# A graph-attention and expert kernel: a small GpSimd fill is put behind every row gather, in a chain

## What is computed

```python
ft = (layernorm(x) @ W).reshape(n, 4, 64)
e = leaky_relu(e_src[src] + e_dst[dst], 0.2)       # a score for each edge and head
a = softmax of e over the edges of one dst, * dist
x = x + segment_sum(ft[src] * a, dst)
x = x + top-2 of 6 experts(layernorm(x))           # three 256x256 layers in each expert
```

## Time and profile before

| what | value |
|---|---|
| median of 3 runs | 4007.06 us (4005.75 to 4013.24) |
| the profiled execution: its own time | 4011.02 us |
| its span, first to last instruction | 4009.3 us |
| mean granted TensorE clock | 0.77 of full speed |
| the gathers of `main_stage` | 1,568, first start at 242.3 us, last at 3124.5 us |
| GpSimd busy over the whole span | 2092.1 us, 52% |

### The profile page before, as it was taken

One profiled execution on the slowest core, in us unless ns is written; L12 is line 12 of the kernel. 1 busy time (PEld: TensorE's weight loads), 2 busy tenths in 40 slices (PEclk: granted clock), 3 DMA queues, 4 the chain that ended last, 5 costly groups with the idle time before them and its releaser, 6 DMA issues. The chain is left out here.

```text
span 4009.3 us, 53462 instructions
## 1 busy us (share of the span) xinstructions
PE 2354.5 (59%) x10832; PEld 1861.4 (46%) x10833; DVE 1938.4 (48%) x4409; ACT 1508.2 (38%) x2731; POOL 2092.1 (52%) x2068
## 2 busy tenths in 40 slices
PE   5733444445544445545455555555556489999995
PEld 4522333333433334434333444444444368777774
DVE  5443344445444445545555565556566683333332
ACT  5612222223332333323333443344444345444443
POOL 0045655555555554554454454444544167777776
PEclk9956667677776777777776776776777789999998
DMA  5433433343433333433333333333433324445453
GB/s 153 161 85 99 107 99 105 102 112 106 110 105 100 110 100 96 112 101 98 100 103 99 96 108 101 101 104 107 113 93 110 92 20 76 79 79 81 80 81 53
DMA packets 231558, 394.55 MB, mean 98 GB/s; under 512 B 55832, under 2 KB 148796, under 8 KB 230881
## 3 DMA queue, kind: packets, MB, share of 16 engines
q0 software_dynamic: 114816, 265.53, 28.2%
q1 hardware_dynamic: 76728, 89.16, 8.3%
q10 hardware_dynamic: 39924, 38.86, 3.0%
HBM read 325.36 MB, written 69.42 MB: 98 GB/s over the span
## 5 line engine op out<-in xcount | busy, mean ns | idle before, releaser
L1001 POOL DMA_INDIRECT m_rows<-table,src_col x1568 | 1498.1, 955 | 1425.8 <-SPq L989 936.6
L1387 PE MATMUL m_A<-m_msg,m_by_edge 128*128 128x260 f32 x3920 | 1313.3, 501 | 1040.4 <-issue 699.8
L1387 PEld LDWEIGHTS m_A<-m_msg,m_by_edge 128*128 128x128 f32 x3920 | 972.6, 256 | 1295.5 <-issue 1096.6
L1085 DVE TENSOR_TENSOR m_msg<-m_rows,m_A 128x2048 f32<-128x2048 f32 (+1 forms) x294 | 568.2, 1933 | 144.3 <-issue 126.1
L1053 DVE TENSOR_REDUCE m_e_sum<-m_E 128x64 f32<-128x192 f32 x295 | 104.8, 355 | 840.7 <-remote 631.8
L1253 ACT ACTIVATE m_z<-m_z 128x32 f32<-128x32 f32 x295 | 67.4, 229 | 1099.8 <-DVE m_z L1064 807.9
L1245 ACT ACTIVATE m_apart<-m_drow,nid 128x1024 bf16 x297 | 340.9, 1148 | 304.5 <-issue 206.2
L1593 POOL DMA_INDIRECT out<-x_con,x_to_i x206 | 329.0, 1597 | 109.2 <-issue 64.9
L1248 ACT ACTIVATE m_by_node<-m_apart,m_one 128x1024 bf16<-128x1024 bf16 x297 | 341.0, 1148 | 11.6 <-issue 1.7
L1046 DVE TENSOR_TENSOR m_by_edge<-m_A,row 128x1024 f32<-128x1024 f32 (+1 forms) x295 | 307.3, 1042 | 60.7 <-issue 57.2
L1760 DVE TENSOR_TENSOR x_con<-x_X,x_b 128x512 f32<-128x512 f32 x103 | 71.3, 692 | 366.4 <-DMA out<-x_con,x_to_i 329.4
(11 more groups left out here) (249 smaller groups left out, 2414.6 us busy)
## 6 DMA issues: line engine op xcount, KB each, us to landing
m_drow<-dst_row SPq DMA_DIRECT2D x196, 256.0 KB
m_rows<-table,src_col POOLq DMA_INDIRECT x1568
table<-f_rowbuf SPq DMA_DIRECT2D x14, 924.0 KB, 5.1
ydram<-m_y ACTq DMA_DIRECT2D x49, 264.0 KB
m_xb<-in_x ACTq DMA_DIRECT2D x48, 256.0 KB
out<-m_x ACTq DMA_DIRECT2D x48, 256.0 KB
f_xin<-in_x SPq DMA_DIRECT2D x13, 896.0 KB, 6.8
x_w<-in_L_ffn_expert_w SPq DMA_DIRECT2D x18, 256.0 KB, 6.0
```

Of the source, the lines that this page charges most:

```text
L1001: nc.gpsimd.indirect_dma_start(rows[:, g % RING, j, :], None, table, bass.IndirectOffsetOnAxis(ap=K.src_col[:, g, j:j + 1], axis=0)).then_ ...
L1085: v.tensor_tensor(msg[i][:, tiles, 0:D].rearrange("p j (h n) -> p j h n", h=HEADS), rws[:, tiles, 0:D].rearrange("p j (h n) -> p j h n", h ...
L1387: m = t.matmul(psA[i][:, 0:ROW], by_edge[i][:, j, :], msg[i][:, j, :], start=(j == tiles[0]), stop=(j == tiles[-1]))
```

## The change

Behind every gather GpSimd fills a scratch tile of 128x128 floats with zeros (`nc.gpsimd.memset`). Nothing reads the tile. Every filling but the first waits until the one ahead of it is complete, on a semaphore of its own. The fills stand in the unrolled program, so there are 1,568 of them and 1,567 waits. Nothing else changes, apart from 64 KB of SBUF that the tile takes.

```diff
+        between_gathers = sb("between_gathers", [P, P])
...
-        gathers_seen = sem("gathers_seen")
+        gathers_seen, spaced_out = sem("gathers_seen"), sem("between_gathers")
...
                     nc.gpsimd.indirect_dma_start(
                         rows[:, g % RING, j, :], None, table,
                         bass.IndirectOffsetOnAxis(ap=K.src_col[:, g, j:j + 1], axis=0)).then_inc(gathered[g % RING], 16)
+                    if g or j:
+                        pool.wait_ge(spaced_out, g * GT + j)
+                    nc.gpsimd.memset(between_gathers[:, :], 0.0).then_inc(spaced_out, 1)
```

## The result

The changed kernel takes 3949.66 us (median of 4 runs, 3929.79 to 3952.18), the one before 4006.4 us (4 runs on the same chip, 4004.52 to 4013.24). The ratio is 0.9848, with a 95% interval of 0.9818 to 0.9878. So the change made the kernel faster, by 57 us where 392 were forecast; the time is inside the forecast's range over all cases and outside that of its likeliest one, in the half-way rival's. The profiled execution took 3929.79 us (span 3928.1), 81 us less than that of before; it is the fastest of the four and 20 us under their median, so what its profile shows as gained is a little more than the 57 us.

A forecast was written before the change was run, and what follows sets the result against it. Bound: main_stage (2883 of 4011 us), where long gather runs starve other engines. POOL's 2289 us plus 200 of pauses make the stage 2490, 393 less, giving 3618, stated as 3615 us; likeliest range 3400 to 3850, over all cases 3400 to 4090.

The forecast's parts named there:

- likeliest one: Whole kernel: most starved stretches go, POOL sets the pace with 200 us of pauses; 3615 us, range 3400 to 3850, chance 0.58.
- half-way rival: In main_stage, starved stretches shrink by a little more than POOL adds: 3850 to 3990 us, chance 0.13.
- What bounds the kernel: In main_stage, long unbroken gather runs take away other engines' instruction starts after some 8 gathers: 950 to 1150 us starved.
- The fills: 1,568 fills on POOL between gathers: each adds its whole 0.204 us, so gathers stand 1.46 us apart instead of 1.257.
- the fill hides in the gap: Between two gathers: they stay 1.257 us apart, time within 8 us of 4007; chance 0.08.
- the two unexplained waits: In main_stage, PE's before m_A and DVE's before m_e_sum: from 690 and 632 us to under 250 each.
- The distance and the starved stretches: In main_stage, gathers 1.46 us apart lengthen the lively part a great deal; most starved stretches go.
- The chained wait: On POOL, fill j waits for fill j-1, which ended a whole gather (0.95 us) earlier; price nothing.
- POOL as a bound: POOL's main_stage work rises from 1971 to 2289 us; under 2883 us POOL by itself makes nothing slower.
- The later gathers: In main_stage a group lands 1.6 us later, covered by the ring of 4 groups except at the stage's end.
- The run counts, not the distance: In main_stage, engines starve whenever gathers follow without real pause; 228 us slower, about 4240 us, chance 0.14.
- POOL becomes the bound: In main_stage, fills cost 0.78 us, gathers 2.04 us apart, POOL needs 3199 us; about 4325 us, chance 0.07.

The follow-up runs named there:

- e1: The changed kernel with fills of 128x384 instead of 128x128, on a starving chip: 3559.1 us, ratio 0.8965 to the kernel before.
- e8: The kernel before, without fills, each gather fetching half rows (half the bytes), on a chip without starvation: 3172.0 us, ratio 1.0007 to the kernel before.
- e11: The changed kernel with fills of 128x272 instead of 128x128, on a starving chip: 3538.8 us, ratio 0.8913 to the kernel before.
- e4: The changed kernel without the chain, fills going to eight tiles in turn, on a starving chip: 3878.3 us, ratio 0.977 to the kernel before.
- e9: The kernel before, unchanged, run again for its profile on a starving chip: 3971.9 us, ratio 0.9996.
- e12: The kernel before, without fills, each gather fetching half rows (half the bytes), on a starving chip: 3978.1 us, ratio 1.0015 to the kernel before.

## Why the prediction was wrong

**What bounds the kernel: right for this chip.** Long gather runs hold up the other engines' instruction starts. e1 removes that, and gives 414 us net of its fills; on the chips on which it isn't there the kernel before is 800 us shorter. One reading was too wide: some 220 of PE's 690 us before `m_A` are there without starvation too (e8). The prediction put the cost at 950 to 1150 us of starved time and the stage without it at 1914 to 2083 us; e8's stage has 2047.

**The fills: the step that failed.** The prediction added the fill's whole duration to the distance of two gathers: "I take the fill by itself, 1.257 + 0.204 = 1.46 us, since the gap stands ahead of every indirect transfer also in `experts` and so belongs to the transfer." The fill's duration was nearly right (0.220 us in the median), the sum wasn't: 0.14 us of the gap goes when a fill stands there. Behind a 128x1 fill of 0.113 us the distance stays 1.258; from 128x128 up it is about 1.12 us plus the fill. The gathers came 1.34 us apart, so only 0.08 of the 0.20 us of spacing was there. The rival "the fill hides in the gap" was right for two thirds of the fill. The text had both bounds, 1.257 and 1.76, and took a value between them; it didn't see that the gap itself can shrink when something stands in it. The gap belonged to the transfer only in part.

At the distance that it assumed the time held: e11, 1.461 us apart, gives 0.8913, which times 4006.4 is 3571 us against the forecast 3615 (an estimate for the first chip, which had gained less than chip 0 from the change). Its sign didn't hold even there: the two unexplained waits were to fall under 250 us each, and e11 has 356 and 289.

**The distance and the starved stretches: direction right, too steep.** "Then a little less inflow lengthens the lively part a great deal." Slot wait on chip 0: 896 us at 1.258, 650 at 1.337, 113 at 1.461. The first 0.08 us took 246 us of it and gave 144 back to the fills; the next 0.12 us took 537 and gave back 208. For each 0.01 us that is 31 us and then 43, so the slot wait falls nearly in step with the distance, a little faster further out; these three points show no sudden edge. The lively part didn't grow: PE is busy 0.34 of the time during the ninth to twelfth gather of a run, where it was 0.33. The time, 3950 us, lies in the half-way rival's range, but this rival was stated for gathers 1.46 us apart. Its number came true with a distance that it didn't have, which is luck; for the distance itself the likeliest case was the better one.

**The chained wait: nothing**, as said; e4 shows it, across two starving chips.

**POOL as a bound: right in kind.** With 128x768 fills it decides (2934 us, 3% over the 2845 of e9's stage), and with 128x384 it alone sets the time. The 200 us of pauses that the sum had were 709 in the change and 113 in e11. The later gathers weren't hidden there, SP waited 59 times, 507.9 us in all, for them, but that costs nothing beyond POOL's own time, since POOL is the bound.

**The rivals.** "The run counts, not the distance" is out: e1's single run of 1,568 gathers starves nobody. "POOL becomes the bound" by fills of 0.78 us is out: they last 0.205 us at least, 0.220 in the median and 0.395 at most, beside a DVE that is busy half the time. Two of them, at 1408.81 and 1410.14 us, last 0.22 and 0.23 us beside DVE's two-input `m_msg`, which takes 2.29 us from 1408.49 us. The Trainium skill ("SBUF — State Buffer", section "SBUF: two separate sides") limits the lock of a DVE operation with two SBUF inputs to GpSimd operations that read SBUF, and by that limit the trace agrees; its other case, DVE in a two-port mode, no run here tested by itself.

**What stays open.** Why a gather instruction holds up the others, whether by GpSimd's work or by the small packets beside it, and why on some chips only. The first chip gained less from the same change (0.985 against 0.977); its fills were 225 ns in the mean against 224 and its distance 1.341 us against 1.337, which is too small a difference to explain it. Between 1.337 and 1.461 us no size was run on a starving chip, and the sizes at 1.550 and 1.870 us ran on another starving chip than those below. The change itself was not run on a chip without starvation; by its own time (2093 us plus about 1,117) it would take some 3210 to 3250 us there, 1 to 3% more than before, an estimate. No version that was run on both kinds of chips beats the kernel before on both: 128x272 fills win 11% on one kind and lose 8% on the other.

## What to carry to other kernels

An operation put into a gap between two instructions can cost less than its duration and more than nothing. Here a fill of 0.22 us in a gap of 0.30 left 0.16 us of the gap standing behind it and cost 0.08 us, while one of 0.11 us left the distance as it was. Price it from both ends, and where the two ends give different answers, give the chance to both. If a kernel shows waits that no semaphore explains, and they come in long runs of one engine's gathers, pace that engine: a few sizes of filler find the point. Here, where it starved, a fill of 0.34 us gave 11% and one of 0.22 us only 2%. Time such a fix on more than one chip before you keep it, for what it cures may not be there on the next.

## What the runs showed that was not expected

The same kernel takes 4006, 3972 or 3168 us on different chips, and nearly all of the difference lies in the stage with the dense gathers. In e8 that stage is 2047 us long and in e12, the same kernel on another chip, 2839 us, with the same 0.952 us for a gather: 792 of the 806 us between the two. PE's matmuls of the stage are busy 1327 us in e8 and 1463 in e12, at a granted clock of 0.81 and 0.71.

A gather of 64 rows lasts 0.911 us and one of 128 rows 0.953, so 64 rows more add 0.042 us, 0.65 ns for each; half the bytes leave it at 0.952. If that holds down to no rows, some 0.87 us are fixed, an estimate. The Trainium skill ("DMA: Bandwidth & Descriptors", section "Anatomy of one DMA — SWDGE (gpsimd) path") says that many descriptors can be emitted before their cost shows; by that the trace agrees.

A fill on GpSimd costs about 0.113 us plus 0.83 ns a column: 113, 220, 282, 340, 436 and 753 ns for 1, 128, 200, 272, 384 and 768 columns.
